# Layer 1's context values made in layer 0's output stage, and a reordered turn in its cross attention

## What is computed

```python
# layer 0, first stage: a gated linear recurrence, its output product, residual and layernorm
x = _layernorm(x + _L0_attn_ref(x, ..., L0_attn_Cm, L0_attn_D), axis=-1)
...
def _L1_xattn_ref(query, key, value, Wq, bq, Wk, bk, Wv, bv, Wo, bo):
    q = proj(query, Wq, bq, Lq)            # 16 heads of 16
    k = proj(key, Wk, bk, Lk)
    v = proj(value, Wv, bv, Lk)            # value is the context: it depends on no layer
    q = apply_rope(q, q_cos, q_sin)
    k = apply_rope(k, k_cos, k_sin)
    scores = jnp.einsum('bhqd,bhkd->bhqk', q, k) * scale
    attn = jax.nn.softmax(scores, axis=-1)
    out = jnp.einsum('bhqk,bhkd->bhqd', attn, v)
    return out.transpose(0, 2, 1, 3).reshape(B, Lq, DIM) @ Wo.T + bo
x = _layernorm(x + _L1_xattn_ref(x, ctx_1024, ctx_1024, ...), axis=-1)
```

## Time and profile before

| | us |
|---|---|
| median of 3 runs (lowest to highest) | 2604.66 (2603.99 to 2605.37) |
| the profiled execution's own time | 2604.75 |
| its span in the profile | 2602.9 |
| PE busy in the span | 2283.5 (88%) |
| DVE, ACT, POOL busy | 1313.6, 908.1, 708.3 |
| stage `yout`, from ACT's first copy to its last | 112.15 to 140.53 |
| stage `x1`, from PE's first product to its last | 726.11 to 872.66 |

### The profile page before, as it was taken

The page is one execution under the profiler, slowest core; times in us unless marked ns, Lnnn a source line. Parts: engine busy times, 40 slices in busy tenths (PEclk is TensorE's granted clock), DMA queues, the critical chain, the costliest instruction groups (busy, mean ns, idle before and its releaser), DMA issues. The chain is left out here.

```text
span 2602.9 us, 48661 instructions
## 1 busy us (share of the span) xinstructions
PE 2283.5 (88%) x18360; PEld 1789.3 (69%) x18369; DVE 1313.6 (50%) x2768; ACT 908.1 (35%) x1591; POOL 708.3 (27%) x1096
## 2 busy tenths in 40 slices
PE   8869999787989999999979988977976889599992
PEld 4647777453567465899968866735865768399992
DVE  4566666698668421111167755553147787511114
ACT  2233333484346301111122225522225667122223
POOL 1722222235223100222212211211324532133332
PEclk9889999898989999999999989988988999799996
DMA  7500000100020100788610002013620000399994
GB/s 282 187 1 1 0 0 1 26 2 0 1 92 2 52 0 1 295 315 315 232 49 0 0 25 73 2 51 89 180 62 5 2 2 3 108 325 326 324 327 138
DMA packets 162729, 253.57 MB, mean 97 GB/s; under 512 B 17296, under 2 KB 123537, under 8 KB 162321
## 3 DMA queue, kind: packets, MB, share of 16 engines
q1 hardware_dynamic: 153360, 230.42, 25.7%
q0 software_dynamic: 9216, 21.06, 3.0%
HBM read 219.79 MB, written 31.13 MB: 96 GB/s over the span
## 5 line engine op out<-in xcount | busy, mean ns | idle before, releaser
L3510 PE MATMUL te_pU<-te_xsT,te_wu 128*128 128x128 f32 x1952 | 233.7, 277 | 1.5 <-DVE te_xsT L3603 1.5
L3510 PEld LDWEIGHTS te_pU<-te_xsT,te_wu 128*128 128x128 f32 x1952 | 231.3, 193 | 5.2 <-issue 2.1
L3531 PE MATMUL te_pY<-te_wd,te_hT 128*128 128x256 f32 x976 | 220.8, 379 | 0.0
L3531 PEld LDWEIGHTS te_pY<-te_wd,te_hT 128*128 128x128 f32 x976 | 180.7, 190 | 22.0
L1230 PE MATMUL x_pB<-early,x_xlT 128*128 128x384 f32 x376 | 133.4, 499 | 1.7 <-ACT x_xlT L1362 1.7
L3560 ACT ACTIVATE te_hT<-te_pU 128x512 f32<-128x512 f32 x78 | 46.6, 597 | 235.0 <-PE te_pU L3510 235.0
L2541 DVE TENSOR_REDUCE x_mx<-x_pR 128x8 f32<-128x1024 f32 x64 | 78.3, 1223 | 78.0 <-PE x_pR L2301 78.0
L3584 DVE COPY te_ys<-te_pY 128x256 f32<-128x256 f32 x61 | 25.9, 425 | 162.8 <-PE te_pY L3531 162.8
L3579 DVE TENSOR_TENSOR te_hT<-te_pU,te_sg 128x512 f32<-128x512 f32 x44 | 30.4, 692 | 147.5 <-ACT te_sg L3558 147.5
L2541 DVE TENSOR_REDUCE a_mx<-a_pR 128x8 f32<-128x1024 f32 x64 | 78.3, 1224 | 44.2 <-PE a_pR L2301 44.2
L3558 ACT ACTIVATE te_sg<-te_pG 128x512 f32<-128x512 f32 x44 | 26.3, 597 | 210.2 <-PE te_pG L3510 210.2
(11 more groups left out here) (669 smaller groups left out, 5624.8 us busy)
## 6 DMA issues: line engine op xcount, KB each, us to landing
te_wu<-in_L_ffn_w_upT SPq DMA_DIRECT2D x39, 1024.0 KB, 5.9
te_wd<-in_L_ffn_w_downT SPq DMA_DIRECT2D x39, 1024.0 KB, 5.8
te_wu<-in_L_ffn_up SPq DMA_DIRECT2D x22, 1024.0 KB, 4.9
te_wg<-in_L_ffn_gate SPq DMA_DIRECT2D x22, 1024.0 KB, 6.9
te_wd<-in_L_ffn_down SPq DMA_DIRECT2D x22, 1024.0 KB, 7.6
moe_first<-in_L_ffn_W SPq DMA_DIRECT2D x8, 1024.0 KB, 8.5
xs_slots<-zeros SPq DMA_DIRECT2D x1, 5120.0 KB, 15.6
ys_slots<-zeros SPq DMA_DIRECT2D x1, 5120.0 KB, 28.9
```

The source lines that it names most:

```text
L3510: ins = pe.matmul(out[g][:, m, :], w[:, k, bass.ts(PER * g + m, P)], xsT[:, k, :], start=(k == 0), stop=(k == KD - 1))
L3531: ins = pe.matmul(pY[u][:, 0, :], hT[:, k, :], wd[u][:, k, :], start=(k == 0), stop=(k == KH - 1))
```

## The change

Three things are changed.

- The value product of the context goes out of `x1` into `yout`. `Wv` gets a buffer of its own, loaded behind `Cm` and `D`; PE makes the 16 value products in eight pairs (`value_pair`) between and behind the four `output` groups, and ACT copies each pair out of PSUM (`store_pair`) into `spare`, a buffer that is now allocated ahead of layer 0 (and lends its room to the first stage's `gl`). In `x1`, `value` is gone on PE and ACT, and POOL's `move_v` adds the bias to a row of `spare`.
- In `yout`, POOL adds D to `core.X` in place, all four groups ahead of the roots.
- In `x1`'s turn: on PE `queries(n+1)` stands ahead of `attend(n-2)`; `turn_back(n-4)` and `output(n-3)` stand ahead of `maxima(n)`. On ACT the copy into `XT` stands behind `copy_normal`. On DVE `scaled(n-4)` stands ahead of `rotate`, and `spread(n-3)` at the turn's end. On POOL the root comes first.

```diff
-        self.x1 = Weights16(self, first, "x1", wq="L1_xattn_WqT", wk=None, wv="L1_xattn_WvT", ...
+        self.x1 = Weights16(self, first, "x1", wq="L1_xattn_WqT", wk=None, wv=None, ...
@@ class Recurrence
+        self.wv = keep.enter_context(nc.sbuf_tensor("values_wv", [P, KD, D], F32))
         sp.dma_start(self.Dt[:], a["L0_attn_D"].partition_broadcast(P)).then_inc(self.out_loaded, 16)
+        sp.dma_start(self.wv[:], a["L1_xattn_WvT"].rearrange("(k p) n -> p k n", p=P)).then_inc(self.out_loaded, 16)
@@ l0_attn_out, gpsimd
             def residual(g):
-                if g >= 2:
-                    pool.wait_ge(r_ready, g - 1)
-                pool.tensor_tensor(xres[g % 2][:], core.X[:, G * g:G * (g + 1), :],
-                                   Dt[:].unsqueeze(1).to_broadcast([P, G, D]), ALU.add).then_inc(xres_ready, 1)
+                x = core.X[:, G * g:G * (g + 1), :]
+                pool.tensor_tensor(x, x, Dt[:].unsqueeze(1).to_broadcast([P, G, D]), ALU.add).then_inc(xres_ready, 1)
...
-            residual(0)
-            residual(1)
+            for g in range(NG):
+                residual(g)
             for g in range(NG):
                 root(g)
-                if g + 2 < NG:
-                    residual(g + 2)
@@ l0_attn_out, tensor
-            for g in range(NG):
-                output(g)
+            def value_pair(v):
+                if v >= len(pV):
+                    pe.wait_ge(v_stored, v - len(pV) + 1)
+                for i in range(2):
+                    for k in range(KD):
+                        ins = pe.matmul(pV[v % len(pV)][:, i, :], core.CT[:, k, bass.ts(2 * v + i, P)], rec.wv[:, k, :],
+                                        start=(k == 0), stop=(k == KD - 1))
+                ins.then_inc(v_ready, 1)
@@ l0_attn_out, scalar
+            def store_pair(v):
+                act.wait_ge(v_ready, v + 1)
+                act.copy(values[:, 2 * v:2 * v + 2, :], pV[v % len(pV)][:]).then_inc(v_stored, 1)
@@ attention16, tensor
             def queries(b):
...
-                    since(pe, v_copied, b - 1)
...
             for n in TURNS:
                 before_first(n)
                 scores(n, 0)
+                if rope and live(n + 1):
+                    queries(n + 1)
                 if live(n - 2):
                     attend(n - 2)
-                if own(n + 1) or rope and live(n + 1):
+                if own(n + 1):
                     queries(n + 1)
...
+                if rope and crossed(n - 4):
+                    turn_back(n - 4)
+                if rope and crossed(n - 3):
+                    output(n - 3)
                 if live(n):
                     maxima(n)
-                if crossed(n - 3):
+                if not rope and crossed(n - 3):
                     output(n - 3)
...
-                if crossed(n - 4):
+                if not rope and crossed(n - 4):
                     turn_back(n - 4)
@@ attention16, vector
-                if crossed(n - 4):
+                if not rope and crossed(n - 4):
                     spread(n - 4)
...
+                if rope and crossed(n - 4):
+                    scaled(n - 4)
                 if rope and live(n + 1):
                     rotate(n + 1)
...
                 if crossed(n - 3):
                     residual(n - 3)
+                if rope and crossed(n - 3):
+                    spread(n - 3)
```

More of the change, by code:

```diff
@@ L186, in __init__ @@
         super().__init__(core, region, name)
-        self.wq, self.wv = (self.take(KD, D) for _ in range(2))
-        self.matrices = [(self.wq, wq), (self.wv, wv)]
+        self.wq = self.take(KD, D)
+        self.matrices = [(self.wq, wq)]
+        if wv:
+            self.wv = self.take(KD, D)
+            self.matrices.append((self.wv, wv))
         if wk:
@@ L939, in l0_attn_out @@
         y = [s.ps(f"y{i}", [P, G, D]) for i in range(2)]
+        pV = [s.ps(f"pV{i}", [P, 2, D]) for i in range(4)]
+        v_ready, v_stored = s.sem("v_ready"), s.sem("v_stored")
         quantized = s.sem("quantized")
```

81 lines of the change are left out of this document (54 added, 27 removed).

## The result

The changed kernel takes 2627.01 us (median of 4 runs, 2624.66 to 2630.48), the kernel before on the same chip 2605.01 (4 runs): a ratio of 1.0082, with a 95% interval of 1.0067 to 1.0097. It is slower, by 22.0 us. The forecast was 2617 with a range of 2605 to 2625, so the direction and the longer turn came out, and the size did not. The profiled execution took 2628.65, its span 2625.7.

A forecast was written before the change was run, and what follows sets the result against it. It took PE and DVE, running in a ring in `x1`, as the bound, lengthened through ACT by the change. `x1` +12.6 and `yout` with what follows +0.4 gave +13.0 on 2604.75: 2617.7, put at 2617 us, range 2605 to 2625.

The forecast's parts named there:

- ring, turns 3 to 14: In `x1`: turns with an `output` take 8.68 us instead of 7.94; 13 turns x 0.74 = +9.6 us, turn 15 included.
- ring, turn 15: In `x1`: the last turn with an `output`, longer by 0.74 us like the others, counted within the +9.6 us.
- turns 0 to 2, and later clock at the start: In `x1`: -1.0 us without the value product ahead of the maxima, +2.0 us for PE's clock rising later.
- falls of the clock in turns 3 to 14: In `x1`: the forecast's sum held no term for PE's clock falling in these turns.
- rest of the tail: End of `x1`: `turn_back(n-4)` ahead of `output(n-3)` sends the last blocks through a neighbour's layernorm; up to 2.8, taken as +2.0 us.
- sum for `x1`: All terms of stage `x1`: 9.6 - 1.0 + 2.0 + 2.0 = +12.6 us.
- `yout`: Stage `yout`: PE's program, with 64 more records, ends the stage; +1.3 to +2.3 us, taken as +1.7.
- clock in `l0_xattn`: Start of `l0_xattn`: PE idles some 4 us, not 14, so its clock may stay up; half of -2.6 taken, -1.3 us.
- The ring: In a turn of `x1`: closed chain of waits through ACT's copies, `output`, maxima and scores, 8.68 us against 7.94.
- rival 3: In `x1`: PE's clock falls or rises late because of its waits; +12 us, about 2630 us; chance 0.06.
- the ring's case: The forecast's own case: in `x1` the chain of waits goes through ACT; 2617 us, own range 2611 to 2625, chance 0.70.
- The start: First turns of `x1`: -1.0 us in turns 0 to 2, +2.0 us (bounds 0 and +5) for a later clock.

The follow-up runs named there:

- filled kernel: Changed kernel with two unused products put into TensorE's turn of `x1` where the value products stood: 2618.34 us, ratio 1.0053.
- the order alone: Changed kernel with values made in `x1` as before and `yout` as before, the new order in `x1` kept: 2618.33 us, ratio 1.0049.
- the values alone: Changed kernel with every engine's order in `x1` as before, values still made in `yout`: 2612.84 us, ratio 1.0020.

## Why the prediction came out as it did

Against the second profile of the kernel before, which entered `x1` at the same time (723.25 and 723.12), the changed kernel's stage is 19.95 us longer. By the prediction's terms:

| term | predicted | measured | how |
|---|---|---|---|
| ring, turns 3 to 14 | +9.6, with turn 15 | +8.8 | 12 x 8.66 against 95.13 |
| ring, turn 15 | in the 9.6 | +1.4 | 5.66 against 4.28 up to `put_maxima` |
| turns 0 to 2, and later clock at the start | +1.0 | +0.7 | 25.75 against 25.02 |
| falls of the clock in turns 3 to 14 | none | +7.2 | turns above 8.66 |
| rest of the tail | +2.0 | +2.1 | 18.77 against 16.70 |
| sum for `x1` | +12.6 | +19.95 | with -0.2 up to the first maximum |
| `yout` | +1.7 | +1.1 to +1.7 | 30.05 and 29.95 against 28.39 and 28.89 |
| clock in `l0_xattn` | -1.3 | -0.7 to +0.5 | 11.41 and 11.38 against 12.04 and 10.94 from there to the first `x_pB` |

- **The ring** was right, step by step, and in sum to 0.02 us, and so was the count of 13 turns: at full clock, turn 15 (5.27 against 4.28) adds 1.0 to the 8.8.
- **The clock** is the step that failed. The sum held nothing for a fall of the clock in the steady turns, and they cost 5.0 and 6.5 us in two profiles, by the filled kernel's and the order's turns. (The 7.2 of the table holds some tenths more, as turn 3 is 8.93 and turn 14 9.03 in the order alone at full clock.) The prediction had put the falls into rival 3, with a chance of 0.06, and argued that "the waits are short and the engine is busy between them". Both are true, as no wait is longer than 1.2 us, and the clock falls all the same, in five and four of the eleven steady turns. The unused products show that without the products' going there are no falls, and the values alone, that their going needs both exchanges beside it. The prediction itself said that the value products lay in the shadow of the maximum of half 1 and that their going would free nothing. The step not taken was to ask of each steady turn, and not only of the first ones, what TensorE would have left between its two new waits.
- **The rival's price** was right in kind: 7.2 us of falls on top of the ring's case is near the 12 that it named, and its 2630 lay 3 us from the result, the range's upper end 2. Its chance was too small.
- **The start.** My -1.0 and +2.0 are +0.7 together by the one profile of before and +2.5 by the other. What the values' going costs at the start stands apart in the run with the values alone: 2.7 to 4.5 us over four turns. So +2.0 was in the bounds of 0 and 5, and on the low side. The -1.0 for the value product ahead of the maxima had no row, and the prediction's own reading, that the product is in a shadow, spoke against it; the order alone, in which the products stay, gains 0.4 us there (24.63 against 25.02), and the values alone lose 1.5 (26.48).
- **The tail** behind the last ring turn came out in size, 2.1 for 2.0, and the steps cost what I had said (4.16 and 3.76 us, for 4.0). Of the range "up to 2.8" I had taken 2.0 without a reason, so the closeness of the sum is in part luck.
- **Stage `yout`** went as read: no stall in the shift, DVE's wait of 3.6 us for the fourth group, and TensorE's program as the end. In the prediction I priced the rule on SBUF in the Trainium skill ("SBUF — State Buffer", Who interferes with whom) at 4 us if nothing took the place of the stall. The trace agrees with the rule (0.16 us for the shift once POOL's additions are out of its way, from 2.23), and the place was taken. The clock there rose earlier than in the kernel before: the earlier trace rows have 0.51 from 112 to 118, the changed kernel 0.76. Of the -1.3 for the clock in `l0_xattn` the profiles show no clear sign (from 142 to 153 the changed kernel has 0.69), and at the start of `x1` nothing of these two terms can be told from the scatter.
- **Not explained:** behind `x1` the changed kernel's two profiles are 1.0 and 3.6 us longer than those of the kernel before, in stages whose code is the same. All profiles lie between 1729.9 and 1733.6 us there, those of kernels that keep the values in `x1` between 1729.9 and 1733.4, so this need not be the change's. With the 19.95 us of the stage the 3.6 make up the difference of the spans (2625.7 and 2602.4). And the start of `x1` lies between 722.3 and 729.1 in the kernels run, of which those that keep the values in `x1` have equal code ahead of it, and most of the others too.

## What to carry to other kernels

Before work is taken off TensorE because it lies in a wait's shadow, ask what its clock does without it: here two products a turn cost nothing in the changed order, and without them some of the same turns took up to 1.6 us longer; in the old order, where TensorE then waited 1.15 us a turn and not 1.91, no steady turn did. A reordering is priced by following one complete ring over all engines, with every join checked for the branch that comes second; where a link is undone, the gain is the lead over that branch and not the link's own length. A stage's tail begins with the last turn of the ring, which has to be counted once, in the one or in the other. An exchange that puts an early result (the maxima) behind a late one (`output`) pays the whole wait in each turn, and one that only fills TensorE ahead of a late operand (queries ahead of `attend`) can be a gain by itself.

## What the runs showed of the hardware

- TensorE's granted clock fell to its lower level (0.51 in one stretch of 2 us) in the midst of work whose longest wait was 1.2 us. It did so late in the stage as well as early, at other turns in each execution, and a fall cost up to 1.6 us of a steady turn.
- Unused products are a means against it: some 0.8 us more of TensorE's work per turn, 8.7 us less time (8.3 by the differences to the kernel before on each chip).
- When the clock rises in the first turns differs between executions of one kernel (8.67 + 6.79 us and 9.60 + 7.66 us for the same two turns).
